# Layer 1 of a Mamba and expert kernel: the transpose of an expert tile's inner rows moved from the end of its slot to the head

## The reference, cut to what matters

```
x = x + _L1_attn_ref(xn, ...) + _L1_ffn_ref(xn, ...)

# _L1_attn_ref: chunked state-space scan (4 batches x 512 tokens, 64 heads of 8, state 128)
proj = xn @ in_proj_w.T ; gate, xBC, dt = split(proj)
xBC = silu(causal_conv4(xBC)) ; x, B, C = split(xBC) ; dt = softplus(dt + dt_bias)
Lmat = exp(segsum(dt * A))                       # the "segment" factor, per head and chunk
y = (C B^T * Lmat) @ x  +  C @ state             # inside a chunk, and from the state before it
out = rmsnorm((y + D x) * silu(gate)) @ out_proj_w.T

# _L1_ffn_ref: 16 experts, top 2 of each token, weights normalised, plus a shared expert
h = silu(x_e @ w1.T) * (x_e @ w3.T)              # 176 inner features, for the tokens of the expert
y = h @ w2.T                                     # times the token's weight, added to its row
```

## Time and profile before

| | us |
|---|---|
| median of three runs | 1239.12 (1238.92 to 1244.82) |
| span of the profiled execution | 1231.4 |
| PE busy in it | 994.4 (81%) |
| DVE busy | 913.8 (74%) |
| ACT busy | 489.7 (40%) |
| POOL busy | 438.8 (36%) |

### The profile page before, as it was taken

The page is one execution under the profiler, slowest core; times in us unless marked ns, Lnnn a source line. Parts: engine busy times, 40 slices in busy tenths (PEclk is TensorE's granted clock), DMA queues, the critical chain, the costliest instruction groups (busy, mean ns, idle before and its releaser), DMA issues.

```text
span 1231.4 us, 18530 instructions
## 1 busy us (share of the span) xinstructions
PE 994.4 (81%) x6024; PEld 580.4 (47%) x6024; DVE 913.8 (74%) x1506; ACT 489.7 (40%) x1114; POOL 438.8 (36%) x333
## 2 busy tenths in 40 slices
PE   3987997787877787765577768999889988899895
PEld 2354555444444444434344534555545554455553
DVE  4658567999999999997486655766768667765576
ACT  2200135555555555540231054544554444544442
POOL 0000101787878877850450103222313222223210
PEclk9989999999999999987788889999998999999998
DMA  6950262788878878977800224333433333334424
GB/s 222 376 146 1 81 130 82 149 153 162 160 147 159 165 148 151 163 136 209 170 6 0 30 83 102 92 84 84 106 89 70 94 88 73 83 84 105 91 40 138
DMA packets 107091, 143.25 MB, mean 116 GB/s; under 512 B 30022, under 2 KB 97334, under 8 KB 102710
## 3 DMA queue, kind: packets, MB, share of 16 engines
q0 software_dynamic: 30368, 77.92, 32.7%
q1 hardware_dynamic: 76630, 64.14, 19.0%
HBM read 72.80 MB, written 39.46 MB: 91 GB/s over the span
## 4 chain that ended last, share of the span: by engine, by line
PE 45%; DVE 18%; DMA 12%; issue 9%; POOL 8%; ACT 6%; ACTq 1%; SPq 0%; DVEq 0%; POOLq 0%
DMA sum<-yo,to_i 9%; PE bank L686 7%; PE bank L1845 4%; PE bank L1427 4%; PE bank L698 4%; PE bank L1434 4%; POOL xg L1171 3%; POOL sum L1164 3%; DVE cv L2090 2%; PE bank L1889 2%; PE bank L1011 2%; PE bank L1875 2%; PE bank L1828 2%; PE bank L1911 2%; PE bank L1028 2%
## 5 line engine op out<-in xcount | busy, mean ns | idle before, releaser
L1499 POOL DMA_INDIRECT sum<-yo,to_i x48 | 77.9, 1622 | 347.1 <-ACT yo L1454 341.6
L1171 POOL DMA_INDIRECT xg<-xn_d,token_i x80 | 97.3, 1217 | 175.2 <-DVE to_i L460 93.7
L1164 POOL DMA_INDIRECT sum<-yo,to_i x80 | 142.5, 1781 | 42.4 <-DMA sum<-yo,to_i 22.0
L1028 PE MATMUL bank<-areaA,hidT 88*128 x320 | 90.8, 407 | 47.6 <-ACT hidT L1076 44.1
L1011 PE MATMUL bank<-areaA,xgT 128*128 x320 | 116.3, 486 | 15.9 <-issue 9.5
L2035 DVE TENSOR_TENSOR areaD<-areaD,gb 128x512 f32<-128x512 f32 x128 | 87.4, 688 | 37.8 <-ACT areaD L1982 37.4
L1982 ACT ACTIVATE areaD<-bank 128x512 f32<-128x512 f32 x128 | 76.1, 595 | 44.1 <-PE bank L1837 43.0
L1028 PEld LDWEIGHTS bank<-areaA,hidT 88*128 88x128 f32 x320 | 54.8, 190 | 77.4 <-issue 73.1
L686 PE MATMUL bank<-xnT,areaB 128*128 128x512 f32 x192 | 86.8, 599 | 0.8 <-DVE y L716 0.8
L1845 PE MATMUL bank<-xnT,w_in 128*128 128x512 f32 x160 | 81.6, 635 | 2.0 <-ACT ecn L1750 1.5
L1489 POOL DMA_INDIRECT xg<-xn_d,token_i x48 | 53.8, 1121 | 82.5 <-DVE to_i L460 68.2
(11 more groups left out here) (341 smaller groups left out, 2198.3 us busy)
## 6 DMA issues: line engine op xcount, KB each, us to landing
y<-xnT POOLq DMA_DIRECT2D x21, 1024.0 KB
wst<-gu_f SPq DMA_DIRECT2D x96, 176.0 KB
y<-areaB POOLq DMA_DIRECT2D x11, 1024.0 KB
wst<-down_f SPq DMA_DIRECT2D x48, 176.0 KB
areaA<-in_gu SPq DMA_DIRECT2D x2, 2816.0 KB
gu_f<-in_gu POOLq DMA_DIRECT2D x1, 5632.0 KB, 17.9
sum<-yo SPq DMA_DIRECT2D x2, 2176.0 KB, 16.3
down_f<-in_down POOLq DMA_DIRECT2D x1, 2816.0 KB, 23.4
```

The source lines that it names most:

```text
L1028: last = nc.tensor.matmul(bank[:, HY, 0:D], hidT[:, q % 2, h, :], wd0_of(e, h), start=(h == 0), stop=(h == 1))
L1164: nc.gpsimd.indirect_dma_start(sum0_d[q % 2], bass.IndirectOffsetOnAxis(ap=to_i[:, q:q + 1], axis=0), yo[:, q % 5, :], None, compute_op=AL ...
L1171: nc.gpsimd.indirect_dma_start(xg[:, q % 5, :], None, xn_d[0], bass.IndirectOffsetOnAxis(ap=token_i[:, q:q + 1], axis=0)).then_inc(s.gathe ...
L1499: nc.gpsimd.indirect_dma_start(sum1_d, bass.IndirectOffsetOnAxis(ap=to_i[:, q:q + 1], axis=0), yo[:, q % 4, :], None, compute_op=ALU.add). ...
```

## The change

In the loop over chunks the parts with `part % 3 == 1`, which are PE's transposes of the inner rows (L1421) with their wait for `hid_ready`, are issued at the head of their slot, ahead of the segment product. The other parts stay at its end. ACT, DVE, POOL and SP are left as they are, and so are the ten projections ahead of the loop. In a slot with parts 0 and 1 the transposes of part 1 now come ahead of those of part 0.

```diff
                 for g in range(G1):
+                    for part in parts_at(n, g):
+                        if part % 3 == 1:
+                            expert_tensor(pe, part)
                     if n < CHUNKS:
                         segment(b, step, g)
                     if n:
...
                     if m is not None:
                         project(b + 1, m)
                     for part in parts_at(n, g):
-                        expert_tensor(pe, part)
+                        if part % 3 != 1:
+                            expert_tensor(pe, part)
```

## The result

| | us |
|---|---|
| before, median | 1239.02 (1237.89 to 1244.82, 4 runs) |
| after, median | 1277.54 (1276.77 to 1278.93, 4 runs) |
| ratio | 1.029, 95% interval 1.026 to 1.032 |

The change costs 38.5 us, 3.1% by the medians, twice what I forecast (+20) and beyond the end of my range (1271). The direction and the place were right; the size was not.

What follows compares the result with a forecast made beforehand. PE was taken to bound the loop over chunks. Hold +23.4, `hidT` wait +2.4 and +0.8, free gaps -1.0, given back -6.0 sum to +19.6 us: 1239.1 to 1259 us, range 1245 to 1271.

Steps and rivals of the forecast that it cites:

- The hold: Slot heads: PE's moved transposes wait for DVE's `hid`, all behind queues; 26.5 us less 3.1 of today's waits, net +23.4.
- The wait for hidT: Down product: its wait does not shrink, as ACT's own order sets the copy; +2.4 with projection, +0.8 with parts 1 and 2.
- What is given back: Later PE waits for DVE, ACT, state and sum of squares swallow some holds: -6.0 us, bounds -3.2 and -15.
- the free gaps: Four slots where the segment product itself waits: the transpose pair goes into that gap, 4 x 0.24 = -1.0 us.
- The clock: Longer PE waits bring none to three more lower-clock stretches, at most 1.7 us each: 0 to 5 us, outside the sum.
- The sign that I gave: Profile after: PE's busy time stays within a few us of before.
- My "worse" case: Rival: the clock falls after each of eight holds above 1.3 us, 13.6 us more, 1273 us; chance 0.08.
- Absorbed: Rival: nearly every hold only replaces a later PE wait, net 0 to +6, about 1242 us; chance 0.12 including nothing.
- Faster: Rival: down product's 20.5 us of `hidT` waits go if ACT's copy follows the early transposes; 1229 us, chance 0.06.
- That nothing happens: Rival: PE reaches the slot head so late that `hid` is always done, no change; within absorbed's chance of 0.12.
- The base: Whole kernel: the median lies 7.7 us above the profiled span, 1231.4 to about 1251 giving 1239.1 to 1259 us.

Runs made afterwards that it cites:

- the long and double sets: Against the kernel before, only the 9 pairs with holds of 1.0 to 1.7 us moved: 1250.4 us; only the 5 in slots with parts 0 and 1: 1248.3 us.
- the small holds: Against the kernel before, only the 12 transpose pairs with holds of 0.36 to 0.73 us moved to the head: 1247.9 us, ratio 1.007.
- the three sets of 26 slots: Three kernels against before, each moving only some pairs: 12 with small holds 1247.9 us, 9 with long 1250.4, 5 in slots with parts 0 and 1 1248.3.
- the 19: Against the kernel before, only the 19 transpose pairs with no hold to expect moved to the head: 1236.2 us, ratio 0.999.

## Why the prediction was wrong, point by point

**The hold** was right in place and nearly in size. I drew 26.5 us from 45 pairs of rows and set 3.1 against it, +23.4. The lists of the loop show 3.3 before and 24.2 after: +20.9. Where the stretch before the slot was not itself changed, single holds came out about as drawn: 1.65 us in slot 14.3, drawn as 1.82, and the free ones near zero. Some differ, because the loop behind a hold no longer runs as before: slot 16.1 2.20 us instead of 1.68, and three slots at n.1 that I had at 0.73 waited 1.3 us (10.1, 14.1, 18.1), as DVE was kept from its weighted x by a PE that came late; slot 20.0 1.69 instead of 2.72.

**The wait for hidT** was right in its direction: +2.2 us measured, +3.2 forecast (2.4 and 0.8). The step in slots with a projection is there to the digit, 0.82 to 1.04 us in slot 16.2; in those with parts 1 and 2 it is smaller than the 0.26 drawn, 0.47 to 0.59 in slot 13.0. The reason given for it, that ACT's own order sets the copy, was shown by moving the copy.

**What is given back** was much less than said. In the loop all of PE's idle time grew by 21.4 us: 20.9 at the transposes and 2.2 at the down product, less 1.7 given back elsewhere. I had put 6.0 there, and 1.0 for the free gaps. In slot 18.1 the hold was 1.33 us and the wait behind it shrank only from 3.35 to 2.77; the two other long waits for `hidT` did not shrink at all (3.40 and 3.40, 2.79 and 2.94). That the sum of these terms, 19.6, stands so near the 21.4 measured is luck in part: hold and `hidT` were 3.5 us too high together, and what is given back 5.3 too high as well.

**The clock** is the step that failed. I left it out of the sum, priced it at 0 to 5 us in the range, and gave more than that a chance of 8 in 100. It was +16.8 us of PE's busy time, and this is why 1277.5 lies above 1271. The sign that I gave, PE's busy time within a few us of before, failed with it. I had the price of one stretch right, half its length: 58.0 - 23.9 = 34.1 us more at half the clock, times 0.5, is 17.1, and 16.8 were measured. The Trainium skill (TensorE: Matmul & The Clock Gate, Terms) gives the same reckoning, the throttled time times the share of pulses that is missing. What was mis-sized is the number of stretches. I allowed for none to three more; there were seven more, and four of the 13 are of double length, against one of six before. My "worse" case was built right, with 8 stretches more for 13.6 us, and even it ends at 1273, 4.5 us short. It should have been in the sum, and the row that I went by could have told me: the stretch of rows 13 does not follow a wait of 3 us. Five of before's six stretches do follow one of 2.7 to 3.4 us, but this one stands behind two shorter waits, in slot 23.2:

```profile
1113.55 0.39 PE L1837 MATMUL bank<-crow,seg_l 94*128 94x512 bf16 x1 [1.41 <-DVE gz_odd L2100]
...
1115.12 1.98 PE L1427 MATMUL bank<-wst,hidT 88*128 88x256 f32 x4 [0.47 <-ACT hidT L1448]
```

**The rivals.** Absorbed: refuted by the result itself, 38.5 us, and by the idle time of the long and double sets; for the small holds it is true by half, and of no help. Faster: refuted, and the point from which it would decide was the right one, since with ACT's copy moved the waits for `hidT` did go. Yet that alone did not bring it below before, because the holds stayed. That nothing happens: refuted for the three sets of 26 slots together, true for the 19.

**The base.** The median lies above the profiled span of before by 7.7 us, which I carried over as a constant. It was not one: for the changed kernel it is 1.9. The profiled execution of before had reached the scan 6.0 us earlier than that of after. As the difference was added to the median, the forecast didn't suffer.

## What to carry to other kernels

An instruction moved to the head of an in-order list takes its wait with it, and everything behind waits too: read for each place when its input is ready, against when the engine would get there, and move only those where it is. Before moving the producer of what a gap waits for, look whether the consumer in between ever waited for that producer (here 2 of 45 times); if not, the list of the engine in between is what to change. And price PE's new waits with the lower clock that follows them: here 21 us of waits brought 17 us more of busy time.

## What was not expected of the hardware

Useless matmuls made a kernel faster: 118 transposes that take 10.4 us of PE's time where nothing is to fill brought the changed kernel from 1277.5 to 1259.9 us. And stretches at the lower clock came also behind waits well below 3 us: in the changed kernel they begin at the 2.20 us of slot 16.1, at the 1.52 us of slot 8.1, and within 1.3 us behind the 1.91 us of slot 9.2 and the 1.34 us of slot 10.1. The set that adds only short holds (no wait for `hid` above 1.0 us in its profile) had a median granted clock of 0.937 over ten runs, beside 0.9415 over 22 runs of before; which waits brought its stretches isn't shown. Times of one kernel follow this clock from run to run: before's 22 runs went from 1232.8 us at 0.945 to 1246.7 at 0.931.
